# The first layer of two attention layers: a load moved behind four copies, the identity loaded from another queue, and a projection computed in one step instead of two

## The reference

```python
q = Wq @ x + bq;  k = Wk @ ctx + bk;  v = Wv @ ctx + bv     # 256 x 512 each, 16 heads of 16 rows
attn = softmax(where(mask, (q * 1/4)^T k, -inf))            # per head 512 x 512
mean = attn @ v;  ex2 = attn @ (v * v);  std = sqrt(relu(ex2 - mean * mean))
xn   = (x - mean_of(x)) / sqrt(var_of(x) + 1e-5)            # masked, along the 512
x    = xn * std + mean
```

## Time and profile before

| | us |
|---|---|
| median of three runs | 1799.29 |
| lowest, highest | 1792.03, 1821.34 |
| the profiled execution | 1799.63 |
| its span, first to last instruction | 1797.8 |
| TensorE busy in it | 1658.3 (92%) |
| DVE, ACT, POOL busy | 1241.9, 1065.8, 516.2 |
| one `maxima` on DVE (256 of them) | 1.222 |
| one `exponentials` on ACT (256) | 1.024 |

### The profile page before, as it was taken

The page is one execution under the profiler, slowest core; times in us unless marked ns, Lnnn a source line. Parts: engine busy times, 40 slices in busy tenths (PEclk is TensorE's granted clock), DMA queues, the critical chain, the costliest instruction groups (busy, mean ns, idle before and its releaser), DMA issues.

```text
span 1797.8 us, 30873 instructions
## 1 busy us (share of the span) xinstructions
PE 1658.3 (92%) x10589; PEld 1125.4 (63%) x10589; DVE 1241.9 (69%) x2758; ACT 1065.8 (59%) x2351; POOL 516.2 (29%) x795
## 2 busy tenths in 40 slices
PE   4899999898898988899999989999999899999999
PEld 2433333333333334788878867888888688888888
DVE  1676767676776764888999889999999863232322
ACT  1366657666565665778877878888888752121111
POOL 0135444446444452232232322223332130000000
PEclk7899999999999989899999999999999999999999
DMA  5445444444444322333223434333333340000000
GB/s 166 124 147 159 148 143 111 139 119 152 138 152 120 97 97 70 85 78 79 70 68 101 117 82 124 89 90 89 92 93 82 94 125 13 1 24 3 21 19 18
DMA packets 112555, 167.97 MB, mean 93 GB/s; under 512 B 27400, under 2 KB 43144, under 8 KB 112272
## 3 DMA queue, kind: packets, MB, share of 16 engines
q1 hardware_dynamic: 88864, 132.61, 25.3%
q0 software_dynamic: 20992, 29.12, 6.5%
q10 hardware_dynamic: 2544, 4.26, 0.9%
HBM read 72.06 MB, written 34.60 MB: 59 GB/s over the span
## 4 chain that ended last, share of the span: by engine, by line
PE 54%; DVE 20%; DMA 10%; issue 6%; ACT 6%; SPq 4%; POOL 0%; ACTq 0%; DVEq 0%; POOLq 0%
PE ps L535 10%; PE ps L1930 9%; PE ps L1904 7%; DMA ring<-top 5%; DVE at_t L1382 4%; DVE at_t L1387 4%; PE ps L1253 4%; PE ps L512 4%; PE ps L1263 4%; PE ps L521 3%; DMA rows<-shares_of 3%; PE ps L1202 2%; PE ps L498 2%; PE ps L1909 2%; PE ps L489 2%
## 5 line engine op out<-in xcount | busy, mean ns | idle before, releaser
L609 DVE TENSOR_REDUCE nmax<-ps 128x2 f32<-128x1024 f32 x256 | 310.8, 1222 | 171.2 <-PE ps L512 169.8
L774 ACT ACTIVATE prob<-ps 128x1024 f32<-128x1024 f32 x256 | 262.2, 1024 | 208.7 <-PE ps L521 205.8
L1590 ACT ACTIVATE at_prob<-at_t,at_nmax 128x256 f32<-128x256 f32 x512 | 256.5, 505 | 86.0 <-DVE at_nmax L1387 72.8
L535 PE MATMUL ps<-prob,v 128*64 128x512 f32 x1024 | 291.4, 649 | 0.4
L1387 DVE CUSTOM_DVE_ANT_0 at_t<-at_t,at_off 128x256 f32<-128x256 f32 x512 | 234.2, 494 | 8.8
L1748 POOL TENSOR_TENSOR at_low<-at_low,at_high 128x512 fp32r<-128x512 f32 x64 | 86.7, 1354 | 465.9 <-DVE at_high L1416 465.9
L2089 DVE CAST mlp_h_hi<-mlp_h 128x512 fp32r<-128x512 f32 x64 | 28.4, 444 | 212.8 <-ACT mlp_h L2001 180.0
L2001 ACT ACTIVATE mlp_h<-ps,b 128x512 f32<-128x512 f32 x48 | 33.1, 690 | 218.3 <-PE ps L1904 218.3
L521 PE MATMUL ps<-ring 64*128 64x512 f32 x512 | 112.4, 432 | 52.2 <-DMA ring<-top 43.7
L512 PEld LDWEIGHTS ps<-ring 64*128 64x128 f32 x512 | 48.8, 188 | 176.0 <-issue 127.8
L1202 PE MATMUL ps<-ident,at_prob 128*128 128x128 f32 x1024 | 157.7, 277 | 0.0
(11 more groups left out here) (218 smaller groups left out, 3938.6 us busy)
## 6 DMA issues: line engine op xcount, KB each, us to landing
ring<-rows SPq DMA_DIRECT2D x62, 512.0 KB, 5.3
rows<-shares_of SPq DMA_DIRECT2D x90, 256.0 KB
at_k_stack<-at_high SPq DMA_DIRECT2D x256, 64.0 KB, 2.5
at_q_stack<-at_high SPq DMA_DIRECT2D x128, 64.0 KB, 2.7
at_q_stack<-at_high POOLq DMA_DIRECT2D x128, 64.0 KB, 2.5
at_q_stack<-at_low SPq DMA_DIRECT2D x128, 64.0 KB, 2.2
at_k_stack<-at_low POOLq DMA_DIRECT2D x128, 64.0 KB, 2.3
c_in<-in_ctx SPq DMA_DIRECT2D x8, 512.0 KB, 6.8
```

The lines of the kernel that those rows point to most:

```text
L535: mm = eng.matmul(ps[2 * QD * k:2 * QD * (k + 1), VB, :], v[:, c, HG * G + 2 * p + k, :], prob[:, M % PROBS, k, :], start=(c == 0), stop=( ...
L609: eng.tensor_reduce(nmax[:, n % 2, j, 2 * p:2 * p + 2], ps[:, at:at + 2, :], AX, ALU.max, negate=True).then_inc(s_max, 1)
L774: eng.activation(prob[:, M % PROBS, :, :], ps[:, ST:ST + 2, :], ACT.Exp, scale=float(HD0) ** -0.5).then_inc(s_exp, 1)
L1590: ins = eng.activation(prob[:, m % 2, i, :], t[:, p, i, :], ACT.Exp, scale=-1.0, bias=nmax[:, m % 4, i:i + 1], accum_out=z[:, T % 2, j, 2 ...
```

## The change

Four places of the first layer change:

- A projection's two halves are computed in one step: the queries' in step 3, the keys' in step 6. Steps 2 and 5 hold none.
- In an odd round SP issues the load of the queries' rows of the next group behind the four copies of the maxima, ahead of the load of the keys' rows.
- SP no longer loads the identity.
- ACT loads it at the start, between `b0` and the first mask.

```diff
     def items_at(w, s):
 
-        if s in (2, 3, 5, 6) and w % 2 == 0 and w // 2 + 1 < PAIRS:
-            return [("q" if s < 4 else "k", w // 2 + 1, ((s + 1) % 3,))]
+        if s in (3, 6) and w % 2 == 0 and w // 2 + 1 < PAIRS:
+            return [("q" if s == 3 else "k", w // 2 + 1, (0, 1))]
...
         eng.dma_start(bv0[:], d["bv0"]).then_inc(s_wv, DMA)
-        eng.dma_start(ident[:], d["ident"]).then_inc(s_ident, DMA)
         rows_in("k", 1)
...
-            if w % 2 and ahead < PAIRS:
-                rows_in("q", 2 * ahead)
             if 0 <= w - 1 < GROUPS:
                 tops_in(w - 1)
...
             if w % 2 and ahead < PAIRS:
+                rows_in("q", 2 * ahead)
                 rows_in("k", 2 * ahead)
                 rows_in("q", 2 * ahead + 1)
                 rows_in("k", 2 * ahead + 1)
...
         eng.dma_start(b0[:], d["b0"]).then_inc(s_set, DMA)
+        eng.dma_start(ident[:], d["ident"]).then_inc(s_ident, DMA)
         eng.dma_start(m_in[:, 0:1, :], d["mask0"].rearrange("b o t -> o b t").broadcast_to([P, NB, D])[:, 0:1, :])\
            .then_inc(s_first_bits, DMA)
```

## The result

The changed kernel takes 1750.8 us (median of four runs, 1749.76 to 1755.58) against 1799.7 for the kernel before: a ratio of 0.9747, 95% interval 0.971 to 0.9785. The profiled execution took 1751.12 us with a span of 1749.3, so 48.5 us less span than before. Forecast were 1759 and a range of 1742 to 1784. Two executions among all that follow, one of the kernel before (3049 us) and one of the run with the later mask (4142.6 us), ran far slower than every other and are left out of all medians and ratios.

A forecast was written before the change was run, and what follows sets the result against it. TensorE was taken as the bound, full in the first layer's loop outside gaps, mainly waits for the maxima. Gains of 19.5 + 9 + 3.9 + 8.3 = 40.7 us gave 1759 us, range over all 1742 to 1784.

The forecast's parts named there:

- Waits for the maxima: TensorE's second product of scores waits less once the queries' load goes behind the maxima: 19.5 us gained (12 to 38).
- The clock: First layer's loop: shorter gaps leave TensorE less time at its low clock, 9 us gained (3 to 16).
- One step for a projection: Six projection matmuls together take 1.61 us, 0.17 less per projection: 3.9 us gained (0 to 5).
- Identity: Start: with the identity early from ACT's queue, round 0's values' product waits only for the bias: 8.3 us gained (5 to 11).
- Cover of the moved load: First scores of w+1: the later queries' load still lands before TensorE wants its rows, no wait added, cost 0.
- Only the start: Waits for the maxima stay nearly unchanged, as the keys' writing ends late and POOL's transfers interfere: 1783 us, chance 0.24.
- Free copies: Small maxima copies pass the keys' writing, or it quickens without a load beside it; waits nearly vanish: 1731 us, chance 0.09.
- Late rows: First scores of w+1 wait in every pair for late queries' or keys' rows: about 1836 us, chance 0.03.

The follow-up runs named there:

- the last run: Changed kernel with queries' rows written before the inverted sums (w%4 = 2), the next batch's mask in step 7, identity behind ACT's first mask: 1762.13 us, ratio 0.9778.

## Why the prediction was right, and where it was off

**The sign and the mechanism held.** The forecast was a sum of 40.7 us; the span fell by 48.5. Step by step:

- *Waits for the maxima, 19.5 forecast.* They fell by 28.9 in rounds 3 to 29 (43.7 less the 2.96 and 0.19 of rounds 1 and 31, against 13.0 less 0.51 and 0.78), 13.7 with w%4 = 3 for 9.5 forecast and 15.2 with w%4 = 1 for 10. But 5 x 1.30 came back as the wait for ACT: 22.4 net. The term was close by two errors that cancel, which is luck. The wait behind the mask was missing: I had asked what the moved load delays, not what the old gap had covered on ACT. What the load's own bytes cost the copies behind the keys' writing, 1.4 us in the forecast, was 1.5 on average in the rounds 7 to 27 with w%4 = 3 (1.6 us behind that end before, 0.1 now). But I took this end as fixed. At w=19 it had come 2.1 us after TensorE's need (412.84 for 410.74), and in the changed kernel the copies behind it are only 1.56 late. At w=21 it had landed 6.1 us after the turning (451.24 for 445.17); now SP waits for no writing when it issues the four loads, the keys' at 419.55, so it had landed within 4.5 us of the turning (415.06). Nothing is left of the waits for w%4 = 1, where I kept up to 1 us each, and 13.0 us are left in all, where I foretold 20 to 25. I also left out that SP itself stood ahead of the queries' load; at w=19 that did not decide.
- *The clock, 9 forecast.* What the odd rounds 3 to 29 gave, 36.6 us, less 22.4, leaves 14 us, and TensorE's busy time in them fell by 14.8. This is the term that was mis-sized, and with the first it makes most of the difference; the mean clock, 0.99 for a forecast 0.98, says the same. I left half of the low clock in place since gaps of up to 3 us would remain. Ten of these fourteen rounds had a mean clock of 0.92 or less before, three have now. The length of the gap alone doesn't sort them: rounds 7, 19 and 27 show 0.91 or 0.92 with gaps of 1.50, 1.56 and 3.51 us, rounds 11, 15 and 23 show 1.00 with 1.44, 1.49 and 2.20. Rounds 19 and 23 of the changed kernel, columns as in the earlier trace rows:

```profile
376.85:396.21 19.36, 17.80 (x86) 7.35 (x85) 13.05 (x20) 10.88 (x13) 13.64 (x18) 0.91 0.79 250
450.38:469.00 18.62, 16.34 (x87) 6.83 (x85) 12.49 (x20) 10.89 (x13) 13.12 (x18) 1.00 0.82 254
```

What else decides it stays open.

- *One step for a projection, 3.9 forecast.* 2.4 in the trace. The 1.61 us were right (1.60), but a step that holds no half any more isn't free of loss: an even round gained 0.25, not 0.34.
- *Identity, 8.3 forecast.* 7.5 in this profile (10.4 with the second profile of the changed kernel), 6.0 when alone. What would be late next was named wrongly: not the bias at 40.5, but the write of the first queries' rows at 41.4. I had the line of code for it before me and gave it no time. The mask came 1.14 us later on ACT (8.17 for 7.03), where I had put 0 to 0.6 and counted nothing; the first writes behind it are late by as much (11.19 for 10.06). How much of that reaches the end is within the spread: with the identity behind the mask (the last run) that write's end frees ACT at 39.54, with it ahead at 41.46 and 38.98 in two profiles.
- *Cover of the moved load, cost 0.* Right: there is no wait at the first scores of an even round in the changed kernel's loop.

**The rivals.** "Only the start" fell with the moved load alone giving 0.9764. "Free copies" fell in the trace: at w=19 TensorE still waited, and 13.0 us are left in all; but its second clause, a writing that gets quicker without a load beside it, fits w=21 above. "Late rows" never came. The Trainium skill's page "DMA: Bandwidth & Descriptors" (Queues, rings and completion order), by which one queue's descriptors are taken in order on each DMA engine, though a later one may finish its write before an earlier one, agrees with the wait that stays at w=19 (1.56 us, and 1.80 where the copies went out earlier) and with the 5.8 us of the sums behind the queries' rows; that the order in the queue alone makes them late, and not the load on the engines, no run here separates.

## What to carry to other kernels

A small transfer that many wait for should be issued ahead of large ones in its queue, and what it is put ahead of, and behind, is read from the queue's own timeline; the order of two neighbours in it was worth 39 us by the median times here, and of what its rounds gave in the changed kernel 14 of 36 us were TensorE's clock. Before counting on a gap's whole length, look at what else waits during it on the engines that the gap covers: at w=21 the next wait took back 1.3 of 2.5 us. And where many engines queue at a start, write down the next wait for each path with its time, not only for the nearest one.

## What the hardware showed unexpectedly

The same four small DMAs did not always cost their engine the same to issue. The copies took SP 2.38 to 3.77 us in the kernel before, 4.48 (w=19) and 5.03 us (w=7) in the run that writes the keys' rows just ahead of them, and on ACT's own queue they took 4.34 us at w=19, 1.08 each, while its first loads took 0.45. And a gap of 2.20 us on TensorE left its clock at full speed in round 23 while one of 1.50 us, in round 7, was followed by the low one.
